# A four-layer gated cross-attention and expert model on one core: slot tiles moved to GpSimd's queue, rank products folded to three, the shared expert cut into eleven groups of 128 features, weights and context loaded from other places

## The reference

```python
x = x + jnp.tanh(g_xattn[3]) * _L3_xattn_ref(_layernorm(x, axis=-1), ctx_2048, ...)
x = x + jnp.tanh(g_ffn[3]) * _L3_ffn_ref(_layernorm(x, axis=-1), ...)
```

```python
shared = _silu_and_mul(x @ shared_gate_up_w.T) @ shared_down_w.T
shared = shared * jax.nn.sigmoid(x @ shared_gate_w.T)
probs = jax.nn.softmax((x @ gate_w.T).astype(jnp.float32), axis=-1)
routing_weights, selected_experts = jax.lax.top_k(probs, TOP_K)
for e in range(E):
    w_e = jnp.where(selected_experts == e, routing_weights, 0.0).sum(-1)
    combined = combined + w_e[:, None] * (_silu_and_mul(x @ w13[e].T) @ w2[e].T)
```

## Time and profile before

| | |
|---|---|
| median of 3 runs | 3363.66 us (3357.4, 3363.66, 3370.97) |
| the profiled execution | 3366.63 us |
| its span in the trace | 3364.9 us |
| mean granted TensorE clock | 0.907 |
| busy: PE | 2767.1 us (82%) |
| busy: DVE | 1700.3 us (51%) |
| busy: ACT | 1175.2 us (35%) |
| busy: POOL | 869.5 us (26%) |
| DMA traffic | 232.33 MB, mean 69 GB/s |

### The profile page before, as it was taken

The page is one execution under the profiler, slowest core; times in us unless marked ns, Lnnn a source line. Parts: engine busy times, 40 slices in busy tenths (PEclk is TensorE's granted clock), DMA queues, the critical chain, the costliest instruction groups (busy, mean ns, idle before and its releaser), DMA issues. The chain is left out here.

```text
span 3364.9 us, 35825 instructions
## 1 busy us (share of the span) xinstructions
PE 2767.1 (82%) x11731; PEld 1704.2 (51%) x11731; DVE 1700.3 (51%) x2977; ACT 1175.2 (35%) x2497; POOL 869.5 (26%) x331
## 2 busy tenths in 40 slices
PE   6998697999653699997899986595899986996695
PEld 3555585644222466554555533573554534775463
DVE  2453675577657898974456544113456544322012
ACT  0111221566515787860143442021244451210110
POOL 0000000588131101000166660102266660410002
PEclk9998898999977799998899988597999997898897
DMA  5130121422100101011312210524321210212423
GB/s 213 63 106 22 69 75 67 105 67 57 51 28 0 51 26 50 26 38 50 87 45 52 57 45 0 218 89 138 87 53 43 57 45 18 102 35 102 149 68 106
DMA packets 104973, 232.33 MB, mean 69 GB/s; under 512 B 22128, under 2 KB 26736, under 8 KB 103408
## 3 DMA queue, kind: packets, MB, share of 16 engines
q1 hardware_dynamic: 99696, 213.59, 20.9%
q0 software_dynamic: 5120, 16.78, 1.5%
HBM read 142.74 MB, written 30.67 MB: 52 GB/s over the span
## 5 line engine op out<-in xcount | busy, mean ns | idle before, releaser
L1450 POOL TENSOR_TENSOR L_attn_total<-L_attn_total,L_attn_probs 128x2048 f32<-128x2048 f32 x120 | 546.7, 4556 | 150.8 <-ACT L_attn_probs L1405 146.2
L1484 DVE TENSOR_REDUCE L_attn_row_max<-L_attn_rows_ps 128x1 f32<-128x512 f32 x512 | 335.5, 684 | 266.8 <-PE L_attn_rows_ps L1291 263.7
L1405 ACT ACTIVATE L_attn_probs<-L_attn_s_ps 128x512 f32<-128x512 f32 x512 | 292.2, 596 | 420.2 <-PE L_attn_s_ps L1311 415.1
L1311 PE MATMUL L_attn_s_ps<-L_attn_q_stack,L_attn_k_stack 98*128 98x512 f32 (+1 forms) x768 | 379.8, 531 | 39.6 <-DMA L_attn_q_stack<-L_attn_ml 34.2
L432 PE MATMUL L_ffn_hidden<-L_ffn_x_high,L_ffn_up_high 128*128 128x512 f32 (+1 forms) x704 | 301.1, 428 | 88.1 <-DVE L_ffn_routes L350 54.1
L316 ACT ACTIVATE L_ffn_sums<-sims 128x128 f32<-128x128 f32 x1024 | 315.4, 389 | 50.3 <-DVE L_ffn_routes L329 26.0
L1450 POOL TENSOR_TENSOR L_attn_total<-L_attn_probs 128x2048 f32<-128x2048 f32 x20 | 92.8, 4638 | 824.1 <-ACT L_attn_probs L1405 824.1
L432 PE MATMUL L_ffn_hidden<-L_ffn_x_low,L_ffn_up_high 128*128 128x512 f32 (+1 forms) x704 | 279.3, 397 | 0.0
L1311 PEld LDWEIGHTS L_attn_s_ps<-L_attn_q_stack,L_attn_k_stack 98*128 98x128 f32 (+1 forms) x768 | 142.3, 195 | 265.6 <-issue 127.7
L1324 PE MATMUL L_attn_o_ps<-L_attn_probs,L_attn_values 128*32 128x512 f32 x1536 | 211.6, 624 | 26.8 <-ACT L_attn_probs L1405 22.9
L453 PE MATMUL L_ffn_y<-L_ffn_down_in,L_ffn_h 128*128 128x512 f32 x512 | 229.1, 593 | 2.0 <-DVE L_ffn_h L554 2.0
(11 more groups left out here) (264 smaller groups left out, 4365.1 us busy)
## 6 DMA issues: line engine op xcount, KB each, us to landing
L_attn_k_stack<-L_attn_kh SPq DMA_DIRECT2D x192, 128.0 KB, 2.4
L_attn_ctxT<-in_ctxT SPq DMA_DIRECT2D x8, 2048.0 KB, 8.0
L_attn_abs_in<-in_L_ffn_w SPq DMA_DIRECT2D x12, 1024.0 KB, 9.7
L_attn_k_stack<-L_attn_kl SPq DMA_DIRECT2D x96, 128.0 KB, 2.4
L_attn_q_stack<-L_attn_qh SPq DMA_DIRECT2D x192, 64.0 KB, 2.0
L_ffn_xg<-x_slots SPq DMA_DIRECT2D x46, 256.0 KB, 2.8
y_slots<-L_ffn_y_sb SPq DMA_DIRECT2D x46, 256.0 KB, 2.0
L_ffn_up_all<-in_L_ffn_w SPq DMA_DIRECT2D x16, 704.0 KB, 15.2
```

Source lines behind the costliest of these rows:

```text
L1311: nc.tensor.matmul(s_ps[:, v % S_SLOTS, :], k_stack[0:depth, n % 2, h, kt * P:(kt + 1) * P], q_stack[0:depth, n % 2, h, :], start=True, st ...
L1405: nc.scalar.activation(probs[:, g % P_SLOTS, h, :], s_ps[:, v % S_SLOTS, :], ACT.Exp, **kinds).then_inc(exp_done, 1)
L1450: nc.gpsimd.tensor_tensor(total[:], first, probs[:, g % P_SLOTS], ALU.add).then_inc(added, 1)
L1484: nc.vector.tensor_reduce(row_max[:, r // HALVES_K, r % HALVES_K:r % HALVES_K + 1], rows_ps[:, r % R_SLOTS, :], AX_X, ALU.max, negate=True ...
```

## The change

Six parts.

1. In attention layers SP issues group 0's weights first, then both halves of the context without waiting between them, each half with a semaphore of its own, then group 1's weights; all in the norm's block, whose end waits for none of these. PE waits for the first half before the first items and for the second after five of them (L0: at each half's first tile).
2. The router's 44 rank products (88 instructions, since each product has two) become 3: three shifted adds on DVE make for every tile the sum of the tiles before it, and one product with `before` and two with `ones` do the rest.
3. `load_x` and `store_y` of `routed_block` go from SP's list to POOL's, ahead of the gathers. PE waits for an expert's up weights before gate and up, and for its down weights before down.
4. L3's shared expert becomes 11 groups of 128 features, with inputs of its own; the loops take an odd number of groups.
5. L3's routed up weights (16 DMAs of 704 KB, 11.5 MB) are issued at the end of SP's list in the shared expert's block, the down weights (16 DMAs, 5.8 MB) at the start of `routed_block`.
6. SP stores each of the 8 tiles of `x` within `routed_block` as its last add is done; `store_block` is gone.

```diff
@@ norm_block @@
+                    load_context(sp, 0)
                     for b in range(BATCH):
                         sp.dma_start(env.ctxT[:, :, b * CTX:(b + 1) * CTX],
-                                     env.io["ctxT"][:, :, b * CTX:(b + 1) * CTX]).then_inc(env.ctx_loaded, 16)
-                        sp.wait_ge(env.ctx_loaded, 16 * (b + 1))
+                                     env.io["ctxT"][:, :, b * CTX:(b + 1) * CTX]).then_inc(env.ctx_loaded[b], 16)
+                    load_context(sp, 1)
...
@@ ffn_block, SP's list, then the loops (the same on every engine) @@
+                    if last_loads:
+                        last_loads(sp)
...
-                with pe.Fori(0, G // 2 - 1) as j:
+                with pe.Fori(0, (G - 1) // 2 - (1 - LAST)) as j:
                     group(2 * j + 1, 1, j + 1)
                     group(2 * j + 2, 0, j + 1)
-                group(G - 1, 1, G // 2)
+                if not LAST:
+                    group(G - 2, 1, G // 2)
+                group(G - 1, LAST, G // 2)
...
@@ expert_weights_block @@
-                for t in range(TILES + 1):
-                    for u in range(min(t, TILES - 1) + 1):
-                        last = nc.tensor.matmul(rank_ps[:, t, :], before[:] if u == t else ones[:], both[:, u, :],
-                                                start=(u == 0), stop=(u == min(t, TILES - 1)))
-                last.then_inc(ranked, 1)
+                rank = rank_ps[:, 0:TILES, :].rearrange("p t e -> p (t e)")
+                nc.tensor.matmul(rank, before[:], both.rearrange("p t e -> p (t e)"), start=True, stop=False)
+                pe.wait_ge(chosen, 2)
+                nc.tensor.matmul(rank, ones[:], earlier[:, 0:TILES, :].rearrange("p t e -> p (t e)"), start=False, stop=True)
+                nc.tensor.matmul(rank_ps[:, TILES, :], ones[:], earlier[:, TILES, :], start=True, stop=True).then_inc(ranked, 1)
...
+                dve.sem_inc(chosen, 1)
+                for n in range(3):
+                    to = earlier[:, 1:, :] if n == 2 else chain[:, n + 1, 4:, :]
+                    link(nc.vector.tensor_tensor(to, chain[:, n, 4:, :], chain[:, n, 4 - 2 ** n:4 + TILES - 2 ** n, :], ALU.add))
...
@@ routed_block, SP's list @@
                 load_weights(sp)
-                sp.wait_ge(slots.scattered, 16 * PICKS * TILES)
-                for i in range(XS):
-                    load_x(i)
-                for i in range(I):
-                    if i + XS < I:
-                        load_x(i + XS)
-                    store_y(i)
+                if out is not None:
+                    for t in range(TILES):
+                        sp.wait_ge(added, PICKS * (t + 1))
+                        sp.dma_start(out[:, t, :], env.x[:, t, :]).then_inc(out_stored, 16)
+                    sp.wait_ge(out_stored, 16 * TILES)
...
                 def down(i, expert):
+                    if i < EXPERTS:
+                        pe.wait_ge(slots.down_loaded[i], 16 * DOWN_LOADS)
                     pe.wait_ge(h_copied, i + 1)
...
@@ streamed_attention_block @@
-                load_weights(0)
                 stack(0)
-                load_weights(1)
...
-                pe.wait_ge(env.ctx_loaded, 16 * BATCH)
+                pe.wait_ge(env.ctx_loaded[0], 16)
                 for n, i in FIRST_ITEMS[:EARLY]:
                     for c in range(DC):
                         chunk(n, i, c)
+                pe.wait_ge(env.ctx_loaded[1], 16)
...
@@ expert_layer @@
-                        ffn_block(env, name, [min(P, E - c) for c in range(0, E, P)], weight, x_parts, meanwhile=route,
-                                  guest=lambda pool: slots.scatter(env, pool))
-                    weights = routed_weights(local)
-                    routed_block(env, name, slots, weights, lambda sp: load_routed(sp, weights), E)
+                        ffn_block(env, name, [P], weight, x_parts, meanwhile=route,
+                                  guest=lambda pool: slots.scatter(env, pool), last_loads=all_up)
+                    down_sb = down_tile()
+                    routed_block(env, name, slots, (up_sb, down_sb), all_down, E, last)
```

More of the change, by code:

```diff
@@ L511, in _ @@
                 group(0, 0)
[L512 removed]
+                with act.Fori(0, (G - 1) // 2 - (1 - LAST)) as j:
                     group(2 * j + 1, 1)
                     group(2 * j + 2, 0)
[L515 removed]
+                if not LAST:
+                    group(G - 2, 1)
+                group(G - 1, LAST, last=True)
             if not ternary:
```

183 lines of the change are left out of this document (114 added, 69 removed).

## The result

| | before | after |
|---|---|---|
| median | 3367.31 us (4 runs, 3357.4 to 3374.47) | 3253.01 us (4 runs, 3245.69 to 3255.15) |
| the profiled execution | 3366.63 us | 3245.69 us |
| its span | 3364.9 us | 3244.0 us |
| mean granted TensorE clock | 0.907 | 0.920 |
| busy: PE, DVE, ACT, POOL | 2767.1, 1700.3, 1175.2, 869.5 us | 2705.8, 1725.0, 1173.0, 918.0 us |

The ratio is 0.9659 (95% interval 0.9627 to 0.969), 114 us less. The forecast was 3245, the range 3228 to 3270. The median of before moved up by 3.7 us with its fourth run. The profiled execution of after is the fastest of its four; the same kernel run again later gave 3251.73 (5 runs, ratio 0.9666, 0.9651 to 0.968) with a profile of span 3250.0, so some 6 of the 120.9 us between the two spans are the luck of one execution.

A forecast was written before the change was run, and what follows sets the result against it. No engine was taken to bound the kernel as a whole, so it was read stage by stage. Terms summing to 119.3 us took the profiled 3366.6 to 3247.3, forecast as 3245 us because that execution lay 3 above the median; range 3228 to 3270.

The forecast's parts named there:

- attention waits: Attention layers L0 to L3: PE no longer waits for a chain of loads on SP; gain 29.9 us.
- clock at their start: First attention products: without the pause PE begins nearly warm; gain 6.2 us for four layers, bounds 0 and 8.
- rank products: Routers of L2 and L3: DVE's waits of 18.05 and 17.78 us nearly vanish; gain 33.4 us.
- slot tiles on POOL: Routed experts: dearer POOL issues, uncovered at three places of 1.0 us each; −3.0 us, bounds 0 and −6.
- shared expert: L3: 12 chunk passes become 11, most of that spent on new waits; gain 2.1 us, bounds 27 and −15.
- L3's routed start: First slot tile no longer behind the weight loads; start falls from 50.2 to 5.5 us, gain 44.7.
- the end: After the last add: tiles stored while DVE adds, leaving 3.1 of 9.1 us; gain 6.0.
- a sign of being wrong: Start of an attention layer: PE's clock at half would show the prediction wrong.
- Rival 2: Attention: context halves share the DMA engines, first half 2 to 4 us late in three layers; 3255 us, chance 0.13.
- Rival 4: Routed experts: GpSimd's queue bounds them; at 5.5 us per load or store 3424 us, slower than before; chance 0.03.
- Rival 3: L3's shared expert: hand-over costs 2 us a group, not 0.5; 3260 us, chance 0.10.
- Rival 1: L3's routed start: first slot tile waits behind 9.6 MB of earlier-issued weights, 27 us not 5.5; 3267 us, chance 0.12.

The follow-up runs named there:

- the last experiment: Changed kernel plus scatter in halves, L3's first slot tiles early, ACT's high halves first, L2's slot tiles and stores and L3's stores on SP: 3221.71 us, ratio 0.9582.
- the run with the early slot tiles: Changed kernel with the scatter in two halves and L3's first three slot tiles issued by POOL before the shared expert's block ends: 3236.28 us, ratio 0.9607.

## Why the prediction was right, and where it was off

The forecast 3245 is 8 us under the median, inside the range; its sum of 119.3 compares with 114 between the medians. Three of the 8 us are the start: the prediction took the profiled execution of before to lie 3 us above the median, and with the fourth run it lies 0.7 below. Term by term, from the two profiles:

| term | forecast | measured | from |
|---|---|---|---|
| attention waits | 29.9 | 29.1 | L0 8.2, L1 8.0, L2 5.2, L3 7.7 |
| clock at their start | 6.2 | 6.7 | 1.9, 2.6, 0.4, 1.8 |
| rank products | 33.4 | 34.0 | first product to `over`: 18.95 twice, now 1.86 and 2.00 |
| slot tiles on POOL | −3.0 | −4.1 | L2 −2.9, L3's last store −1.2 |
| shared expert | 2.1 | 3.4 | 207.4 to 204.0 |
| L3's routed start | 44.7 | 42.0 | 50.2 to 8.2 |
| the end | 6.0 | 5.7 | 9.1 to 3.4 |
| not foreseen | 0 | −2.0 | gathers beside stores −0.9, L3's routed stage −1.1 |
| sum | 119.3 | 114.8 | |

The attention waits are measured from the norm's first transpose to the first product. The two spans differ by 120.9, so the terms leave 6.1; 3.8 of them lie in L2's attention, where single executions differ anyway.

- **Attention starts.** Right, mechanism and size, and the undoing shows it: 27 us. The clock was right in sum and wrong in place. In L1 and L3 the norm's tiles are turned in one go and PE enters the layer at its higher level. L2's norm turns two tiles every 5.4 us (its rows have 8 transposes, then 3.4 us of idleness), at a granted clock of 0.50, so PE comes in at the lower level whether it has paused or not, and gained 0.4 us, not 2.8. The prediction had named that as a sign of being wrong, and it came in one layer of four; that the sum still came out, with 1.9 us in L0 and 2.6 in L1, is in part luck. Rival 2 did not come: PE's first product follows ACT's last copy by 0.6 us in all four layers.
- **Rank products.** Right, in both layers, shown by the trace and by the undoing (33 us).
- **GpSimd's queue.** Rival 4 is dead by a price: 0.54 us for a plain load or store, where I had allowed 1.3 by the indirect ones, so 1.1 us for a tile of 6 to 8. The Trainium skill's rule ("SBUF — State Buffer", section "SBUF: two separate sides") that GpSimd's transfers look blocked while DVE runs certain fast copies was not put to the test: each store is issued 0.3 us after DVE's copy of its tile has ended, and not one of POOL's plain issues in the two routed stages stands beside an instruction of DVE. That L2 lost 2.9 instead of 2.0 has a part I had not seen: after the last add of L2 the next block begins 3.0 us later (DVE's idle time ahead of L3's norm), where it was 1.4. With these transfers on SP's queue the next block begins after 1.4 us again, and L2's stretch is back at 204.2, as before the change (203.9).
- **Shared expert.** The wait of 9.4 behind the scatter and the half microsecond of each group are in the profile to the tenth, and PE begins slowly behind the wait, as foretold. The wait at the end is 2.5 us, not 1.6. Rival 3 (2 us a group) did not come. That the gain of a chunk pass goes into waits was the finding, and the last experiment takes most of it out again.
- **Routed start.** The step that was mis-sized: I let the first slot tile land in 4.5 us after a microsecond of issue, and it takes 6.5; block hand-over adds 1.7. Neither row that I took the 4.5 from is of this case: 2.8 us is the median of slot tiles with little beside them, 3.5 that of the first load of a stream, with nothing in front. Rival 1 (behind everything that was issued) did not happen on GpSimd's queue: the tile lands 2.0 us before an up load that was issued 12.5 us earlier on SP's, and in the run with the early slot tiles 11.4 us before one that was issued 4.2 us earlier. Within SP's queue rival 1's rule does hold: the tile landed 0.7 us behind the last up load where few of them were left, and 12.8 us after its issue with 16 down loads in front. (Rival 1's 9.6 MB should be 9.0, by the prediction's own figures: 17.3 less 8.3.) The Trainium skill's rule that transfers of all issuing engines run on the same 16 DMA engines and interleave ("DMA: Bandwidth & Descriptors", section "Issuing engines are not separate DMA queues") agrees with that: the tile shares the engines with the loads beside it and takes 6.2 to 9.5 us on GpSimd's queue. The remark in the same section of the Trainium skill, that another issuing engine saves only the sequencer's time, "which is usually small", does not carry over: behind the down loads SP came to the slot tile 13.8 us late, needing up to 1.6 us for an issue, and the overtaking comes on top. So GpSimd's queue gives two things, a list without weight loads in it and a way past what SP has issued.
- **The early up loads** I had counted within that term as needed. They were not: issued late they cost nothing, so part 3 alone brings the whole 42 us. Part 5 alone brings about half: with the up loads early and the slot tiles behind the down loads on SP's queue, PE's pause is 27.9 us instead of 51.5.

## What to carry to other kernels

When a stage starts with small loads behind large ones, move the small ones to the front of the list or to a queue without the large ones; preloading the large ones as well may add nothing, so try each alone. When groups get smaller, count what else stands in the lists of the helper engines: a burst of 20 us that hid in a group of 50 does not hide in one of 17, and the order on the engine that prepares operands begins to show. A change whose parts are each undone alone soon shows which parts carry it.

## What the runs showed of the hardware

- To issue a plain 256 KB load or store takes 0.54 us on POOL's queue, an indirect one 0.95 to 1.4 us and 0.3 between two.
- With the DMA engines full, SP's issues stretch from 0.38 to 0.47 us (the first four down loads) to as much as 1.9 us, in the run with late up loads to 4.3, and the 16 down loads take 13.2 to 17.7 us.
- Loads on SP's queue land in the order of issue, up to 23.5 us after it when 11.5 MB are issued at once. A slot tile on POOL's queue passes them: issued 4.2 us after an up load it landed 11.4 us before it.
- A 256 KB load on POOL's queue issued beside 17.3 MB of weight loads lands in 6.3 us, and beside little a slot tile lands in 2.7 to 3.2.
- Behind a block whose slot tiles went over POOL's queue the next one begins later: DVE's idle time ahead of L3's norm is 3.0 us, and 1.4 with these transfers on SP's queue.
- PE's granted clock stood at 0.50 of 2.4 GHz, its lower level, in a pause of 8.2 us (3016 to 3020), and the first eight transposes behind it took 2.2 us; behind a pause of 1.3 us, in the last experiment, they took 1.35.
